# A macaron block on one core: four first FFNs before the first second one, side chains dealt over all tiles in single steps, one add moved to GpSimd, four hidden buffers

## The reference

```python
x = x + 0.5 * ffn(layernorm(x))                  # the first FFN
x = x + mixer(layernorm(x))                      # a gated convolution and a scan over time
x = x + 0.5 * ffn(layernorm(x))                  # the second FFN, with the same weights

def ffn(h):                                      # 32 experts of width 64, 4 of them chosen
    scores = sigmoid(h @ router_weight.T); sfc = scores + router_bias
    # 4 groups of 8 experts; a group counts by the sum of its two best sfc; the best 2 groups stay
    # of these the 4 best experts; their scores, divided by their sum, times 2.5, are the weights w
    out = sum_e w[e] * down_w[e] @ (silu(gate_w[e] @ h) * (up_w[e] @ h))
    return out + shared_down @ (silu(shared_gate @ h) * (shared_up @ h))    # shared expert, width 128

def mixer(h):                                    # D = 128, 5 taps, per sequence
    gate, val = split(h @ W_in.T)
    u = sigmoid(gate) * (conv5(val) + conv_b)
    y[t] = tanh(a_param) * y[t-1] + u[t]
    return layernorm(h + y @ W_out.T) * ln_w + ln_b
```

## Time and profile before

| what | value |
|---|---|
| median of 3 runs | 722.85 us (722.22 to 723.27) |
| the profiled execution | 722.28 us, its span 720.5 us |
| PE busy | 667.3 us, 93% |
| DVE busy | 582.6 us, 81% |
| ACT busy | 419.5 us, 58% |
| POOL busy | 477.4 us, 66% |
| DMA | 78.84 MB, mean 109 GB/s |
| granted TensorE clock, mean | 0.992 of full speed |

### The profile page before, as it was taken

The page is one execution under the profiler, slowest core; times in us unless marked ns, Lnnn a source line. Parts: engine busy times, 40 slices in busy tenths (PEclk is TensorE's granted clock), DMA queues, the critical chain, the costliest instruction groups (busy, mean ns, idle before and its releaser), DMA issues. The chain is left out here.

```text
span 720.5 us, 10391 instructions
## 1 busy us (share of the span) xinstructions
PE 667.3 (93%) x3016; PEld 523.0 (73%) x3016; DVE 582.6 (81%) x1547; ACT 419.5 (58%) x801; POOL 477.4 (66%) x709
## 2 busy tenths in 40 slices
PE   5579999998989999989999899999999899999997
PEld 5457786777766777867877677776777678777785
DVE  4778697788978878887797978989698887978765
ACT  4436665664655566566656565655665565665553
POOL 1147767865677767777667775777676866687673
PEclk9899999999999999999999999999999999999999
DMA  8492907408464290833909075370916428090370
GB/s 194 96 208 56 216 1 160 93 1 180 88 147 91 51 213 19 182 71 85 182 23 212 18 163 105 83 155 20 221 28 145 108 66 173 13 216 24 86 167 16
DMA packets 60010, 78.84 MB, mean 109 GB/s; under 512 B 7696, under 2 KB 27184, under 8 KB 59952
## 3 DMA queue, kind: packets, MB, share of 16 engines
q1 hardware_dynamic: 59424, 77.91, 50.2%
q10 hardware_dynamic: 528, 0.26, 0.2%
HBM read 75.01 MB, written 3.15 MB: 108 GB/s over the span
## 5 line engine op out<-in xcount | busy, mean ns | idle before, releaser
L487 POOL TENSOR_TENSOR hid_lo<-hid,hid_hi 128x256 fp32r<-128x256 f32 x540 | 389.9, 746 | 199.9 <-ACT hid_hi L584 199.0
L584 ACT ACTIVATE hid_hi<-hid 128x512 fp32r<-128x512 f32 x272 | 170.6, 627 | 125.1 <-DVE hid L735 123.1
L722 DVE TENSOR_TENSOR weighted<-gate_ps,raw 128x512 f32<-128x512 f32 x256 | 175.1, 684 | 67.1 <-ACT gate_ps L576 54.3
L576 ACT ACTIVATE gate_ps<-gate_ps 128x512 f32<-128x512 f32 x256 | 148.5, 580 | 97.8 <-PE gate_ps L1010 94.5
L735 DVE TENSOR_TENSOR hid<-weighted,up_ps 128x512 f32<-128x512 f32 x256 | 174.7, 682 | 13.8 <-DVE weighted L722 0.5
L1053 PE MATMUL down_ps<-hid_hi,wt_hi 128*128 128x512 f32 x272 | 108.6, 399 | 5.8 <-ACT ffn_sb L588 5.7
L1056 PE MATMUL down_ps<-hid_lo,wt_hi 128*128 128x512 f32 x272 | 107.9, 397 | 0.2 <-DVE hid_lo L743 0.2
L1054 PE MATMUL down_ps<-hid_hi,wt_lo 128*128 128x512 f32 x272 | 107.7, 396 | 0.0
L1008 PE MATMUL up_ps<-xT_hi,wt_hi 128*128 128x512 f32 x187 | 77.9, 417 | 12.2 <-DVE hid L735 11.9
L1008 PE MATMUL gate_ps<-xT_hi,wt_hi 128*128 128x512 f32 x187 | 80.3, 430 | 5.7 <-DVE weighted L722 5.6
L1010 PE MATMUL up_ps<-xT_hi,wt_lo 128*128 128x512 f32 x187 | 74.4, 398 | 0.0
(11 more groups left out here) (148 smaller groups left out, 1083.8 us busy)
## 6 DMA issues: line engine op xcount, KB each, us to landing
raw<-wT_hbm SPq DMA_DIRECT2D x64, 640.0 KB, 13.3
raw<-wT_hbm SPq DMA_DIRECT2D x32, 512.0 KB, 7.6
raw<-wT_hbm SPq DMA_DIRECT2D x32, 256.0 KB, 4.1
x_res<-in_L_attn_x SPq DMA_DIRECT2D x8, 256.0 KB, 5.3
x_ln<-in_L_attn_x SPq DMA_DIRECT2D x7, 256.0 KB, 13.9
out_x<-x SPq DMA_DIRECT2D x7, 256.0 KB, 2.3
raw<-in_L_ffn_gate_w SPq DMA_DIRECT2D x4, 256.0 KB, 5.4
raw<-in_L_ffn_up_w SPq DMA_DIRECT2D x4, 256.0 KB, 5.0
```

The costliest lines, as they stand in the source:

```text
L487: last = nc.gpsimd.tensor_tensor(hid_lo[s][:, cols], hid[s][:, cols], hid_hi[s][:, cols].bitcast(F32), ALU.subtract)
L576: nc.scalar.activation(bank[:, :] if j else silu_sb[:, :], bank[:, :], ACT.Silu).then_inc(silu_done, 1)
L584: nc.scalar.activation(hid_hi[s][:, :], hid[s][:, :], ACT.Copy).then_inc(hid_hi_done, 1)
L722: V.tensor_tensor(weighted[j % 2][:, :], gate_ps[n % BANKS][:, :], wb[:, j - 1, :], ALU.mult)\
```

## The change

- Four first FFNs stand at the head (AHEAD = 4), so a block's side chains have more units between its two FFNs. ORDER is (1,0) to (1,3), then (4,b), (1,b+4) by turns, then (4,4) to (4,7).
- The tables are new. ADD, PROJECT, MIXER and NORM4 take the place of CHAIN and the old NORM4, and a block's chain between its FFNs runs over three units.
- The routing is 26 single steps, spread evenly by `even(2, 12)` over slots 2 to 12; its end, and "weights", move from slot 12 to slot 13.
- Five small routing buffers move from SBUF to free columns of the PSUM bank `routed`.
- The add x2 moves from DVE to POOL. `x1` has two buffers, the hidden ring four.
- On PE the first down product of a unit moves from tile 3 to tile 4 (tile 3 then has none and tile 4 has two).
- Some steps that DVE ran at j + 0.5, behind `hid` of the tile, stand at j, ahead of it: the router's first read, "add ffn 1", "xT low 2", "mixer sum".

```diff
-ORDER = [(1, 0), (1, 1), (1, 2)] + [f for b in range(NBLK - 3) for f in ((4, b), (1, b + 3))]
-ORDER += [(4, NBLK - 3), (4, NBLK - 2), (4, NBLK - 1)]
-RING = 3
+AHEAD = 4
+ORDER = [(1, b) for b in range(AHEAD)] + [f for b in range(NBLK - AHEAD) for f in ((4, b), (1, b + AHEAD))]
+ORDER += [(4, b) for b in range(NBLK - AHEAD, NBLK)]
+RING = 4
...
-            return k == 1 and b == 1 or k == 4 and b % 2 == 1
+            return b % 2 == 1 and (k == 4 or k == 1 and b < AHEAD)
...
-        x1 = sb("x1", [P, TT, P])
+        x1 = [sb("x1_0", [P, TT, P]), sb("x1_1", [P, TT, P])]
...
-        n_best = sb("n_best", [P, TT * NG])
-        far_single = sb("far_single", [P, TT * NG])
+        n_best = routed[:, 388:388 + TT * NG]
+        far_single = routed[:, 404:404 + TT * NG]
         best1_tied = sb("best1_tied", [P, TT * NG])
-        best_other = sb("best_other", [P, TT * NG])
-        best2 = sb("best2", [P, TT * NG])
+        best_other = routed[:, 420:420 + TT * NG]
+        best2 = routed[:, 436:436 + TT * NG]
...
-        grank = sb("grank", [P, TT * NG])
+        grank = routed[:, 452:452 + TT * NG]
...
+        def even(first, last, n=ROUTE):
+
+            return tuple(first + int(i * (last - first) * 2 / (n - 1) + 0.5) / 2 for i in range(n))
...
+        PROJECT = {"stats 2": 1, "meanvar 2": 1.5, "norm 2": 2, "normalise 2": 3, "transpose 2": 9, "xT high 2": 9,
+                   "xT low 2": 9, "mixer gate": 11, "tanh gate": 11, "mixer value": 12, "copy value": 12,
+                   "add ln_b": 15}
...
+        NORM4 = {"meanvar 3": 0, "norm 3": 0, "normalise 3": 1, "scale 3": 2, "x2": 10, "stats 4": 12,
+                 "meanvar 4": 13, "norm 4": 14, "normalise 4": 15}
...
+                  "xT high 4": 7, "xT low 4": 7, "router 4": 9, "silu logits 4": 10, "route 4": even(9, 13),
+                  "weights 4": 14}
...
             if k == 1:
-                return (at(NORM4, b - 1) + at(ROUTE4, b - 2) + at(OUTPUT, b - 3)
-                        + (at(NEXT, b + 1) if b < NBLK - 1 else []))
-            return at(CHAIN, b + 2) + at(PREPARE, b + 3)
+                return (at(MIXER, b - 2) + at(XT4, b - 3) + at(ROUTE4, b - 3) + at(OUTPUT, b - 4) + at(NEXT, b + 1))
+            return at(NORM4, b + 1) + at(PROJECT, b + 2) + at(ADD, b + 3) + at(PREPARE, b + 4)
...
+                    for b in due(steps, "x2", j):
+                        pool.wait_ge(x1_b_done, b + 1)
+                        pool.wait_ge(scaled_done, b + 1)
+                        if b >= 3:
+                            pool.wait_ge(ffn_added[4], b - 2)
+                        nc.gpsimd.tensor_tensor(x2[b % 3][:, :, :], scaled[:, :, :], x1_b[:, :, :], ALU.add)\
+                          .then_inc(x2_done, 1)
...
-            def route_logits(k, b, st):
...
+            def route_step(k, b, st, n):
+
+                if n == 0:
+                    dve.wait_ge(logits_ready[k], b + 1)
+                    return st.done(V.tensor_scalar(tiny[:, :, :], side_te, -1e-9, 1e-8, ALU.is_ge, ALU.mult))
+                if n == 3:
+                    dve.wait_ge(logit_silu_done[k], b + 1)
                 st.wait()
...
-                    if j >= LAG:
+                    if j == LAG + 1:
+                        down(k, m, 0)
+                    if j > LAG:
                         down(k, m, j - LAG)
```

More of the change, by code:

```diff
@@ L274, in macaron_kernel @@
         x3_free = sem("x3_free")
+        ROUTE = 26
         def at(table, b):
             return [(name, slot, b) for name, slot in table.items()]
[L286 to L322, removed]
@@ new lines, in macaron_kernel @@
+        XT4 = {"transpose 4": 0, "xT high 4": 0, "xT low 4": 0.5}
+        ROUTE4 = {"router 4": 2, "silu logits 4": 3, "route 4": even(2, 12), "weights 4": 13}
+        OUTPUT = {"copy ffn 4": 2, "transpose ffn 4": 5, "halve ffn": 5, "add ffn 4": 8}
+        PROJECT_0 = {**PROJECT, "stats 2": 5, "meanvar 2": 6, "norm 2": 6, "normalise 2": 7}
+        TAPS = {"conv": (14, 14.5, 15, 15.5, None, None)}
+        MIXER_0 = {**MIXER, "conv": (None, None, None, None, 0, 0.5), "y high": 1, "y low": 1, "mixer out": 5,
+                   "mixer sum": 5, "stats 3": 6}
@@ L761, in xT_low, with by_group @@
                  .then_inc(xT_lo_done[k], 1)
[L764 to L778 removed]
+            def by_group(t):
+                return t[:, :, :].rearrange("p t (g c) -> p t g c", g=NG)
@@ L884, in recur, with chain_at, beside @@
                 assert st.n == MIX
-            def beside(slot, steps, routing, mixing):
+            def chain_at(sem, b, length, part):
+                st = Steps(dve, sem, b * length)
+                st.n = part
+                return st
+            def beside(slot, steps):
                 for b in due(steps, "stats 1", slot):
@@ L951, in unit @@
                         weigh_tile(k, m, j)
-                    beside(j, steps, routing, mixing)
+                    beside(j, steps)
                     hidden_tile(k, m, j)
@@ L955, in unit @@
                         last_hidden_low(first_tile(k, m) + j - 1)
-                    beside(j + 0.5, steps, routing, mixing)
+                    beside(j + 0.5, steps)
             const = Steps(dve, dve_const, 0)
@@ L969, in _ @@
                 if n == 3:
-                    route_logits(1, 0, first)
+                    for step in range(3):
+                        route_step(1, 0, first, step)
                 weight_low(n)
@@ L975, in _ @@
             dve.wait_ge(pool_const, 5)
-            for part in range(PARTS):
-                for n in range(4 + 2 * part, min(6 + 2 * part, NBATCH)):
-                    weight_low(n)
-                route_part(1, 0, first, part)
+            for step in range(3, ROUTE):
+                if step % 2 and 4 + step // 2 - 1 < NBATCH:
+                    weight_low(4 + step // 2 - 1)
+                route_step(1, 0, first, step)
             dve.wait_ge(x_ln_loaded, 32)
```

207 lines of the change are left out of this document (94 added, 113 removed).

## The result

The changed kernel takes 712.81 us (median of 4 runs, 710.14 to 713.38); the kernel before took 722.54 us beside it (721.5 to 723.27). The ratio is 0.9864, 95% interval 0.984 to 0.9888. The gain is 9.7 us where 22.8 were forecast; the sign held, and the range (690 to 713) by 0.2 us.

What follows compares the result with a forecast made beforehand. PE, 93% busy, was taken as the bound, with 57 us of stalls to gain. First five units -16.8, steady pairs -7.7, last five units +1.7 and setup 0 sum to -22.8 us, giving 700 us; range 690 to 713.

Steps and rivals of the forecast that it cites:

- All gain is stalls of PE: Whole kernel: the matmuls stay the same, so only PE's stalls, 57 us of the span, can be gained.
- The burst in the routing: Routing on DVE: `best_tied` and the next step fall to near 0.18 us; up's two stalls per pair, 1.3 us each, go.
- The adverse price on `gdiff` and `beats`: Routing: these two keep two SBUF inputs and may wait for POOL, taken as 0.4 us each, costing PE nothing.
- The first five units: Units (1, 0) to (4, 0): 209.4 us instead of 226.1, a change of -16.8 us, bounds -20 and -6.
- The steady pair: Pair (4, m), (1, m): 82.3 us against 84.9, with a new 2.4 us stall in (4, m); three pairs -7.7 us.
- The down product: First down product one tile later: takes away waits for ACT's copy, 1.7 us steady and 3.3 in the first five units.
- x2: Add moved to POOL: 0.97 us off DVE, some 1.3 us onto POOL, at no cost there.
- rival A: Walk too pessimistic, since the fourth ring buffer lets DVE and ACT run ahead of POOL: 689 us, chance 0.14.
- The last five units: Units (1, 7) to (4, 7) with the tail: 212.0 us against 210.3, +1.7 us, bounds -4 and +7.
- rival C: Slower: steps ahead of `hid` make DVE wait for side matmuls within a tile: 724 to 732 us, chance 0.08.
- rival B: Steady units gain nothing, only the first five units gain, and the end loses 4 us: 710 us, chance 0.18.
- late weights: Weights at slot 13 may reach DVE late: nothing in the steady part; 3 us allowed in the range's upper end.

Runs made afterwards that it cites:

- experiment 3: The changed kernel with the five small routing buffers back in SBUF: 712.9 us, ratio 0.986 to the kernel before.
- experiment 4: The kernel before with only the five small routing buffers moved to PSUM: 715.51 us, ratio 0.9911 to the kernel before.
- experiment 2: The changed kernel with the last block's chain one unit earlier: 707.94 us, ratio 0.9801 to the kernel before.
- experiment 9: The changed kernel with only the distances in the end's tables widened (normalises two tiles behind norms, last transposition and router later): 703.26 us.
- experiment 10: The changed kernel with the end's distances widened and the last block's chain one unit earlier, steady units' tables untouched: 692.96 us.
- experiment 1: The changed kernel with norm 2 at tile 4 instead of 2 and normalise 2 at tile 6 instead of 3, wherever PROJECT's values serve: 700.86 us.
- experiment 5: The changed kernel with the add x2 back on DVE at the same slots: 708.12 us, ratio 0.98 to the kernel before.
- experiment 6: The changed kernel with the first down product of a unit at tile 3 again: 710.81 us, ratio 0.9841 to the kernel before.
- experiment 7: The changed kernel with three hidden buffers instead of four: 711.89 us, ratio 0.985 to the kernel before.

## Why the prediction was right, and where it failed

- *All gain is stalls of PE.* Right: the matmul count and the pace at full clock are unchanged, and the differences found are waits, restarts or the clock.
- *The burst in the routing.* Right in mechanism and size (168 and 170 ns beside "near 0.18"); in the three steady pairs the waits of up for `hid` are down to 1.3 us, none over 0.4:

```profile
PE gate_ps L993 <- DVE weighted L728: 3.2, 4, 1.0
PE up_ps L993 <- DVE hid L741: 1.3, 3, 0.4
```

  The adverse price on `gdiff` and `beats` (0.32 us each, 0.4 taken) is absorbed, as said. What I didn't see is that with the new tables the PSUM columns carry no time (experiment 3); in the old order they were worth 6.5 us (experiment 4).
- *The first five units.* Right: -16.1 us beside -16.8, unit by unit 42.4, 41.1, 43.8, 40.4 and 42.3 us beside 41.7, 41.3, 43.2, 40.7 and 42.6 by the count of work and the stalls foreseen. That it is within 0.7 us is partly luck: in experiments 2, 9 and 10, which leave these units alone, they take 208.0, 211.4 and 209.5 us, and the 3.1 us of low clock in (1, 0) were in no term.
- *The steady pair.* Right: 82.2 us beside 82.3, with the stall at the tile, of the size and by the chain foreseen, though the longer wait is at the gate product and not at up; experiment 1 takes it away.
- *The down product, x2, the ring.* x2 cost nothing in the steady part, as said; at the end its part stays open (experiment 5). The down product's move was credited with 1.7 and 3.3 us, most of which the tables take away without it (experiment 6). That was inside terms that came out right, so the miss isn't here. The hidden ring's fourth buffer, a reason for rival A, is worth nothing measurable (experiment 7).
- *The last five units: the step that failed.* "Sum 212.0 against 210.3: +1.7 us. Bounds: -4 and +7." It measured +15.3, outside its bounds. Only the steady pair was walked through engine by engine; for the first and the last five units a stall per unit was set down, and here the stalls are too small. The mechanism that the walk had found for (4, m), a normalise one tile behind its norm with the silu behind it in ACT's queue, stands in these units too, and in (1, 7) with `xT low 2` ahead of `hid`, which is rival C's mechanism in one place. My count had 4.6 us of stalls in (4, 6), and there are 11.5, 3.0 of them clock. Of the 13.6 us missed, 4.6 are low clock behind the long waits, which no term had, and the other 9.0 are waits and restarts. Experiments 2, 9 and 10 show both halves, the crowded last chain and the distances: by medians 4.9 and 9.6 us alone, 19.9 together. Their gains don't add, so no share can be given to each.
- *The range.* That 712.81 lies in it is luck. Its upper end stood for steady units that gain nothing (rival B) and 3 us for late weights. The steady units gained 7.9 us, and DVE waited 10.1 us for the weights where it had waited 11.7; the loss at the end brought the time there.

What stays open is what exactly decides whether the clock falls behind a wait: of the four waits of PE over 1.8 us in the changed kernel three were followed by the low clock and the longest, of 3.03 us, was not, while in the kernels of experiments 2 and 7 the same wait was. And the 4.7 us by which experiment 5's median is lower aren't explained.

## What to carry to other kernels

When a schedule is new in all its stages, walk the first and last stages as carefully as the steady one: here they hold more than half of the time, and the last nearly all of the error. Leave room (here two tiles did, where one did not) between an operation on a slow engine and the one that needs it on an engine whose queue also feeds TensorE, and put no operation that waits for another engine ahead of one that TensorE waits for. Price a wait of TensorE of 2 us at up to 3.5, since the clock can fall behind it. Look at unit lengths, not at the sum alone, when two fixes are tried apart: together they may give more than their sum. And ask of each unit that changed whether its own tables did: if not, it may be the clock.
